# A decoder of two layers on one core: the turned maxima in another bank of PSUM with fewer waits, and GpSimd's weight pieces one place earlier

## The reference

```python
    x = x + _L0_attn_ref(_layernorm(x, axis=-1), ...)     # local attention in buckets of 64, then an MLP with GELU
    x = x + _L0_xattn_ref(_layernorm(x, axis=-1), ctx_1024, ctx_1024, ...)   # cross attention, rotary
    x = x + _L0_ffn_ref(_layernorm(x, axis=-1), ...)      # attention, then a mixture of 8 experts, top 2, and a shared one
    x = x + _L1_attn_ref(_layernorm(x, axis=-1), ...)     # retention with decay and a group norm
    x = x + _L1_xattn_ref(_layernorm(x, axis=-1), ctx_1024, ctx_1024, ...)   # cross attention in a causal window of 64
    x = x + _L1_ffn_ref(_layernorm(x, axis=-1), ...)      # a mixture of 16 experts, top 2 of 2 groups, and a shared one
```

```python
        scores = jnp.einsum('bshd,bthd->bhst', q, k) * scale
        attn = jax.nn.softmax(scores, axis=-1)
        ctx = jnp.einsum('bhst,bthd->bshd', attn, v).reshape(B, S, d)
```

## Time and profile before

| what | value |
|---|---|
| median of 3 runs | 1462.07 us (1457.41 to 1466.78) |
| the profiled execution | 1464.77 us |
| its span, first to last instruction | 1462.9 us |
| TensorE busy | 1298.5 us, 89% of the span |
| VectorE, GpSimd, ScalarE busy | 59%, 48%, 39% |
| granted TensorE clock, mean | 0.953 of full speed |

### The profile page before, as it was taken

How to read it: one execution, slowest core, us unless ns; L and a number is a source line. 1 busy time by engine, 2 the same in 40 slices (tenths; PEclk the granted TensorE clock), 3 DMA queues, 4 the chain that set the end, 5 groups by cost and what they waited for, 6 DMA issues and landing times.

```text
span 1462.9 us, 33803 instructions
## 1 busy us (share of the span) xinstructions
PE 1298.5 (89%) x12132; PEld 1045.0 (71%) x12132; DVE 867.4 (59%) x2050; ACT 571.1 (39%) x1272; POOL 705.6 (48%) x949
## 2 busy tenths in 40 slices
PE   5999979988999999979889999959998999818897
PEld 4666647876777777758889999846765777617776
DVE  4888743337888888736512121158875778773346
ACT  2555535523444455643222222214443555413331
POOL 5566632017667466630223333237784556427426
PEclk9999968998999999989999999979999999958999
DMA  6000000020000000000298999630000000028964
GB/s 252 2 2 0 2 1 30 1 86 16 13 15 5 2 16 15 16 16 1 80 338 314 334 325 328 245 137 30 0 16 9 25 28 26 16 92 284 316 189 144
DMA packets 47370, 137.79 MB, mean 94 GB/s; under 512 B 6925, under 2 KB 29646, under 8 KB 41104
## 3 DMA queue, kind: packets, MB, share of 16 engines
q1 hardware_dynamic: 32944, 110.37, 21.4%
q0 software_dynamic: 7536, 19.67, 4.4%
q10 hardware_dynamic: 6768, 6.16, 1.2%
HBM read 119.54 MB, written 17.56 MB: 94 GB/s over the span
## 4 chain that ended last, share of the span: by engine, by line
PE 61%; DVE 14%; DMA 10%; issue 8%; POOL 5%; ACT 1%; DVEq 0%; SPq 0%; POOLq 0%; ACTq 0%
PE ps L1159 11%; PE ps L1018 8%; PE ps L967 7%; PE ps L1292 7%; PE ps L1066 5%; DMA back_of<-w_odd 4%; DMA row_in<-rows_of,from_u 4%; PE ps L1304 3%; PE ps L1035 3%; PE ps L1044 3%; DVE negmax L1734 3%; PE ps L911 2%; PE ps L958 2%; PE ps L1073 2%; PE ps L993 2%
## 5 line engine op out<-in xcount | busy, mean ns | idle before, releaser
L1292 PE MATMUL ps<-hT,w_tile 128*128 128x128 f32 x1624 | 199.9, 278 | 8.4 <-DMA w_tile<-in_w_f 7.4
L1292 PEld LDWEIGHTS ps<-hT,w_tile 128*128 128x128 f32 x1624 | 190.6, 194 | 12.6 <-issue 7.1
L1358 ACT ACTIVATE probsT_all<-ps 128x1024 f32<-128x1024 f32 x128 | 131.1, 1024 | 158.3 <-PE ps L967 158.3
L1734 DVE TENSOR_REDUCE negmax<-ps 128x8 f32<-128x1024 f32 x128 | 155.9, 1218 | 54.2 <-PE ps L967 53.9
L967 PE MATMUL ps<-qe,kf 32*128 32x256 f32 x1280 | 152.9, 386 | 0.0
L967 PE MATMUL ps<-ke,qf 32*128 32x256 f32 x1024 | 143.6, 398 | 0.0
L747 POOL TENSOR_SCALAR eps_sum<-mv 128x1 f32<-128x1 f32 x112 | 25.4, 227 | 201.0 <-DVE mv L1671 169.4
L967 PEld LDWEIGHTS ps<-qe,kf 32*128 32x128 f32 x1280 | 110.4, 189 | 4.9 <-issue 2.7
L2255 DVE TENSOR_TENSOR h_in<-ps,act_sb 128x512 f32<-128x512 f32 x39 | 27.0, 691 | 143.3 <-PE ps L1292 143.3
L1066 PE MATMUL ps<-probsT_all,va 128*32 128x128 f32 x2560 | 104.4, 281 | 6.1 <-ACT probsT_all L1358 4.4
L691 POOL DMA_INDIRECT back_of<-be,to_u x39 | 39.4, 1010 | 144.7 <-DVE be L2268 144.7
(11 more groups left out here) (266 smaller groups left out, 3226.8 us busy)
## 6 DMA issues: line engine op xcount, KB each, us to landing
w_tile<-in_w_f SPq DMA_DIRECT2D x39, 1536.0 KB, 9.3
w_tile<-in_w_f SPq DMA_DIRECT2D x47, 385.0 KB, 7.3
back_of<-w_odd ACTq DMA_DIRECT2D x47, 128.0 KB
ctxT<-in_ctxT SPq DMA_DIRECT2D x32, 128.0 KB, 2.1
rows_of<-nv SPq DMA_DIRECT2D x32, 128.0 KB, 1.7
w_even<-in_w_att SPq DMA_DIRECT2D x3, 1024.0 KB, 7.2
y_back<-back_of SPq DMA_DIRECT2D x6, 512.0 KB, 5.0
x_all<-in_x SPq DMA_DIRECT2D x4, 512.0 KB, 10.6
```

What stands on the lines that cost most here:

```text
L1292: last = mm(ps[:, 2 * which + at.two, fc * P:(fc + 1) * P], w[:, col:col + P], rowT[:, at.two, c, :], start=c == 0, stop=c == KC - 1)
L1358: nc.scalar.activation(half_of(probsT_all, half), ps[:, 2:4].rearrange("p b n -> p (b n)"), ACT.Exp, scale=HD ** -0.5).then_inc(S["probs"], 1)
L1734: nc.vector.tensor_reduce(m, ps[:, 0:2].rearrange("p b (h k) -> p (b h) k", h=HB), AX.X, ALU.max, negate=True).then_inc(S["s_max"], 1)
```

## The change

`turn_maxima` writes to the first 128 columns of bank 2, the first bank of the scores by key, in place of bank 7, and `inject` reads them there. Its waits for the values (`va_sb`) and for the residual of two tiles before (`x_done`) go; a wait for the probabilities of the tile before (`probs`, both halves) comes. `project_values` no longer waits for `inj_sb` of the tile before. On GpSimd `first_low(at)` is called before `norm_low(normed(at))`, after `norm_base`.

```diff
                 norm_base(normed(at))
+                first_low(at)
                 norm_low(normed(at))
-                first_low(at)
...
                 last = tile.back(1)
                 wait(pe, "va_sb", last)
-                if last is not None and last.l != RET and tile.l != RET:
-                    wait(pe, "inj_sb", last)
...
             def turn_maxima(tile):
                 wait(pe, "nm_sb", tile)
-                wait(pe, "va_sb", tile)
-                out = tile.back(2)
-                wait(pe, "x_done", tile.back(3) if out is not None and out.l == RET else out)
-                tr(ps[:, B_V, 0:P], nmx[:], ident).then_inc(S["m_out"], 1)
+                wait(pe, "probs", tile.back(1))
+                tr(ps[:, 2, 0:P], nmx[:], ident).then_inc(S["m_out"], 1)
...
-                tt(inj[:], ps[:, B_V:B_V + 1, 0:P].to_broadcast([P, HB, P]),
+                tt(inj[:], ps[:, 2:3, 0:P].to_broadcast([P, HB, P]),
```

## The result

| | kernel before | changed kernel |
|---|---|---|
| median of 19 runs each | 1465.82 us (1457.41 to 1475.28) | 1457.54 us (1447.49 to 1464.73) |
| the profiled execution | 1464.77 us | 1454.22 us |
| its span | 1462.9 us | 1452.4 us |
| granted TensorE clock, mean | 0.953 | 0.956 |

The ratio of the times is 0.995, with a 95% interval from 0.993 to 0.9971: 0.5% less, some 7 us (4 to 10). The forecast was 1455.4, 6.7 us under the median known then. In the changed kernel the lines behind the edits have other numbers: the turn L1052 is L1048, L1749 is L1745, L1762 is L1758, L1777 is L1773, L1864 is L1860, L1850 is L1846, L1893 is L1889, L1088 is L1084, L1066 is L1062, L1073 is L1069. GpSimd's lines keep theirs.

A forecast was written before the change was run, and what follows sets the result against it. TensorE, busy 89% of the span, was taken as the bound, so edits pay only where it idles. Terms of -2.9, -2.0, -2.6, +1.5, +0.3 and -1.0 sum to -6.7 us: 1455.4 us from median 1462.07, range 1447 to 1464.

The forecast's parts named there:

- A: XATT0: the turn no longer waits for the residual and starts up to 0.33 us earlier a step; -2.9 us.
- The prediction's marks: Signs in XATT0: no idle time before the turn, period some 0.25 us shorter, L1850's wait near 0.2.
- The turn in ATT0: ATT0: the turn comes 0.42 us earlier, but TensorE's idle time moves to before the scores; zero, bounds 0 and -0.4.
- The added and the removed waits: Attention steps: the new wait and the other removed ones are met on arrival; zero each, bounds 0.1 us in all.
- B: End of ATT0: pieces move into GpSimd's idle time, so VectorE's second L1749 is no longer blocked; -2.0 us.
- C: End of ATT0: the granted clock's first fall gone, the second still there; -2.6 us, 7.0 if neither comes.
- D: First piece of ATT1: the moved piece blocks VectorE's L1749 and delays what follows; +1.5 us, bounds 0 and +2.0.
- XATT1 (+0.3): First piece of XATT1: it falls on VectorE's small gate work; +0.3 us, bounds 0 and +1.0.
- E: Last piece of ATT1: the root comes about 1.1 us earlier and TensorE's wait for `nv` goes; -1.0 us.
- Rival (1): The clock holds through the end of ATT0: -11.7 us, 1450.4 us; chance 0.22.
- rival (2): Nothing arrives: XATT0's gain becomes another wait, the clock falls as before; -1.2 us, 1460.9 us; chance 0.16.
- rival (3): Slower: pieces block VectorE in ATT1 and XATT1, and the clock falls near 613 us; +2.6 us, 1464.7; chance 0.10.

The follow-up runs named there:

- e7: Kernel before, with identity turns filling TensorE's waits in the last two tiles of ATT0, ATT1 and XATT1; 0.9941 of the kernel before.
- e12: Kernel before with TensorE's waits filled by identity turns, plus GpSimd's pieces ahead of the normed block's low half; 0.9923 of the kernel before.
- e1: Kernel before with the turned maxima in bank 2 and the changed waits, GpSimd's pieces left in place; 0.9974 of the kernel before.
- e3: Changed kernel with the first piece of each layer behind the low half again; 0.9964 of the kernel before.
- e5: Changed kernel run again without any edit, for a second profile; 0.9944 of the kernel before.
- e6: Changed kernel with the first piece put back and identity turns filling TensorE's waits; 1447.21 us, 0.989 of the kernel before.
- e11: Changed kernel with the turn's wait for the values and the values' wait for `inj_sb` put back; XATT0's second to sixteenth turn 129.25 us.
- mask-first runs: VectorE's masked maxima moved ahead of the following norm's variance, in the filled changed kernel with first piece back (0.9873) and in the kernel before (0.9963).
- the two filled kernels: Identity turns in TensorE's waits, in the kernel before (0.9941) and in the changed kernel with the first piece put back (0.989).
- e2: Kernel before with only GpSimd's pieces moved ahead of the normed block's low half; 0.9998 of the kernel before.
- e4: Changed kernel with the residual's wait put back ahead of the turn, still in bank 2; XATT0's second to sixteenth turn 133.15 us.

## Why the prediction came out right, step by step

**The turn in XATT0 (A, -2.9 us): right in mechanism, too small.** The seven profiles with the wait for the residual have c between 133.15 and 133.45, the seven without it between 129.00 and 129.38: -4.0 us, past my bound of -3.6. The idle time went as I had counted it: 3.8 us before the fourteen turns, of which 0.7 stay, so 3.1 go, for 2.9 forecast. What I had wrong is the moment at which the turn can start. I took the end of the queries for it (425.21). In the changed kernel the turn starts ahead of that end in twelve of the fourteen steps, by 0.12 to 0.16 us and 1.9 us in all: 416.38, while the queries run to 416.55 (the ends of matmuls are modelled in the profile, the starts are not). So a matmul that waits for nothing overlaps the one ahead of it, and one behind a wait does not; counted idle time leaves that out. From the start of the last query's matmul to the start of the instruction behind the turn, the fourteen steps take 4.5 us in place of 9.6; of these 5.2 us the stage keeps 4.0. Where the rest goes wasn't looked for. The prediction's marks came true: no idle time in most steps, a period 0.29 us shorter (0.25 forecast), L1846 without its wait.

**The turn in ATT0 (0).** The turn came 0.4 us earlier and TensorE then waited for `inj`, as forecast. Of the thirteen steps (a) the first depends on the clock at the kernel's start (9.5 to 10.4 us). Where it is 9.5, a is 145.24 and 145.29 us with the wait for the residual (e7, e12) and 144.82 to 144.96 without it (e1, e3, e5, e6, e11): 0.4 us less, at my bound. So the idle time was moved, as I had it, but for 0.03 us a step. The mask-first runs showed how little is to be had there: behind the wait for `inj` stands one for the maxima.

**The added and the removed waits (0).** Right: e11_waits_back is the changed kernel in every stage, and the new wait for `probs` shows in no row.

**The pieces at the end of ATT0 (B, -2.0).** Right: 2.01 us for the two tiles when the clock is the same in both (e12 against e7). The Trainium skill (SBUF — State Buffer, Who interferes with whom) has the tensor_scalar in a two-port mode stand behind GpSimd's instruction in full; the traces agree, with 1.19 us behind the piece of 1.27 and 1.73 us behind that of 1.82, and 0.17 in the open, though no row tells the mode.

**The clock there (C, -2.6).** The step behind it was the weak one: it took the clock's falls of one execution for a property of the waits. Second profiles of the same kernels had them elsewhere. In b the kernel before gives 46.8 us on average and the changed one 43.1 (two and three profiles, with half clock over 19 to 29 and 15 to 21 us); 2.3 of these 3.7 us stand between the two filled kernels over the two tiles (22.81 against 20.51), where the clock is held, so some 1.4 us would be the clock's. The edited kernels give more: the three unfilled profiles with the pieces behind (these two and e1) have a mean of 47.2, the six with them ahead (the three and e2, e3, e4) 42.6, with half clock over 25.5 and 18.0 us on average. Of these 4.5 us 2.0 are the pieces', and 2.5 would be the clock's. Yet in the whole hardly anything of it is seen: the mean granted clock is 0.9547 over 29 executions of the changed kernel and 0.9543 over 43 of the kernel before that ran beside the later experiments. So in b the clock gave something between 1 and 3 us in these profiles; that the kernel keeps it isn't shown. What neither fall would cost was put at 7.0; filling gave 7.6 in the kernel before.

**The first piece of ATT1 (D, +1.5).** Right in place and mechanism, the size was +1.0 (26.0 to 27.0 in every profile, back at 25.9 with the piece back). I had made every following step as late as the blocked one. But the turn had stood behind TensorE's own queries, and of L1745's 1.56 us more only 0.38 appeared before it and 0.42 before the scores. In XATT1 (+0.3) the CAST L2001 was blocked for 0.79 us in place of 0.17, and nobody waited for it: its last three steps took 29.24 us with the pieces ahead and 29.25 with them behind (e12 and e7), and 29.1 in the changed kernel by its turn.

**The last piece of ATT1 (E, -1.0).** TensorE's 1.01 us before the turn of `nv` went. With filled waits in both, e went from 18.22 to 17.61, so -0.6. Unfilled, the clock hides the gain or more than takes it: e lies between 17.6 and 22.9 us with the pieces ahead (20.1 on average), and between 18.9 and 19.7 with them behind (19.2). Whether the new order also makes a fall there likelier (half clock before 636 us in three of six unfilled profiles with the new order, in none of the four with the old one) stays open.

**The sum.** Without the clock: -4.0 - 0.4 - 2.0 + 1.0 - 0.2 (XATT1, by its turn) - 0.6 = -6.2 us, where the medians say -8.3 and the ratio -7.3 (4 to 10 less). So 1 to 2 us are left for the clock, and the interval is wider than that. Three other comparisons bear the terms out: without D the sum is -7.2, and e6 against e7, with the clock held in b, gave -7.8; the turn alone should give -4.6 and gave -3.9 (e1, between -7.4 and -0.4); the pieces alone should give -1.6 and gave -0.3 (e2, between -3.3 and +2.8), so that the runs don't show the pieces' move to pay as a whole. The mechanisms of A, B, D and E were right. That -6.7 came so near is partly luck: A was 1.1 too small, D and the 0.3 of XATT1 together 1.0 too dear (XATT1's last steps even won 0.2), and E and, by the whole's measure, C were too large. Rival (1) fell, as a fall remained in all unfilled profiles; rival (2) because A arrived in full; rival (3) because A and B arrived, and behind the first piece of ATT1 no fall came before 22 us later (599.95 and 624.4).

## What to carry to other kernels

When a wait is for a bank and not for the data, move the result to a bank whose last reader has already been waited for: the gain was the idle time and 30% more (4.0 us for 3.1), since a matmul without a wait also overlaps the one ahead of it, and it came only in the stage where no later wait stood right behind. Before you move an elementwise piece of work on GpSimd, look what VectorE does in the same 2 us, for each place of the move: of the places costed here, the ends of ATT0 and of ATT1 gained, XATT1 cost nothing, and the first piece of ATT1 cost 1 us. Never read a stretch at half clock from one profile as the effect of an edit: take a second one of the same kernel, or fill TensorE's waits and compare at full clock; filling the waits was worth as much as the change.

## What the runs showed of the hardware

- A matmul without a wait starts before the modelled end of the one ahead of it (the turn at 416.38 us, the queries' end at 416.55); behind a wait it doesn't, and that came on top of the idle time: 1.9 us in fourteen steps.
- The clock's falls aren't reproducible from execution to execution: with the same waits of 1.04 and 0.85 us the granted clock stayed at 1.00 in one profile of the changed kernel and fell to 0.50 at 188.0 us in another. The Trainium skill (TensorE: Matmul & The Clock Gate, Part 1) says of the start of a kernel that the same kernel measures different numbers of slow matmuls from run to run. The first step of ATT0 agrees, with 9.92 us in one profile of the kernel before and 10.26 in the other; and the traces show the same of the falls in the middle, which come first at 187.4 and 192.9 us in the kernel before and at 197.7 and 188.0 us in the changed one.
- 49 turns of the identity in waits of 0.6 to 2.9 us kept the clock at 1.00 from the fourteenth tile of ATT0 to the MLP, and with 34 in each of the two other layers filled they made the changed kernel 0.5% faster again (0.989 against 0.9944, the first piece's 0.07% included). The Trainium skill (TensorE: Matmul & The Clock Gate, Part 4: PE-mode transpose) has it that a transpose in that mode does not count as activity for the clock in the same way. The fp32 turns here (`nc.tensor.transpose`, in the rows MATMUL with the identity) did keep the clock up, since nothing but such turns was added; whether the mode was on no row tells. With 59 of them in ATT0, in the kernel before with the pieces ahead, a fall of 6.9 us came all the same.
- A short VectorE instruction that starts 0.11 to 0.12 us behind a GpSimd tensor_tensor ends with it (0.17 us becomes 1.19 or 1.73); the one behind it starts 0.11 us behind GpSimd's next instruction and ends with that one (0.18 becomes 0.65).
